# Who waits for the scatter of a mixture-of-experts stage: SyncE on one semaphore, or GpSimd on four

## The chip, the cores and the metric

One NeuronCore of a Trainium2 chip runs the whole program. The metric is the device time of one execution in microseconds. The kernel before takes 1391.34 us (median of 3 runs, 1389.32 to 1392.08).

## The reference, cut to what matters

Four layers run one after the other over 2048 tokens of width 256, each with layer norms and a residual around it: attention, a mixture of experts, a state-space layer, a feed-forward layer. The change is in the second one:

```
logits = flat @ router_w                       # 2048 x 64
_, topk_idx = top_k(logits + router_bias, 4)   # four experts per token
routed = sum over the 4 choices of share * expert(token)
shared = sum over s of (silu(flat @ swg[s]) * (flat @ swu[s])) @ swd[s]
out    = routed + shared
```

## The kernel before

`stage_moe` has two parts, `stage_route` and `stage_slots`, and each is one `nc.Block()`: five programs, one per engine, that run side by side and talk by semaphores. At the end of a block all engines meet: each drains and signals, GpSimd collects the signals of the other four after its own program has ended, and releases them. Line 782 is that of the route block, line 1169 that of the slots block.

In `stage_route` the 16 token tiles (`NT`) of 128 rows are normalised into `rows`, the router picks 4 experts (`TOPK`) per token, and VectorE works out in `find_slots` a row number for each of the 2048 x 4 choices, in four groups of tiles; each group raises `slots_ready`. GpSimd then copies the rows into the DRAM tensor `slots_in` (`xs` in the code), which SyncE had filled with zeros: 64 indirect DMAs (line 826), one per tile and choice, each of 128 rows of 1 KB. Each adds 16 to the semaphore `scattered`. These DMAs are the last work of GpSimd's program in this block. SyncE's program issues the constants' loads and nine blocks of zeros, and then waits until `scattered` is 1024 (line 790).

TensorE, ScalarE and VectorE meanwhile compute the shared experts: 16 steps of `hidden` (lines 897) into `pg` and `pu`, gate (line 967), product (line 1081), split (lines 971, 1085) and `down` (line 907) into `acc`. TensorE runs the first four steps as straight code and the other twelve as a loop of three passes (`repeat`); the other two engines have straight code throughout. Beside steps 3 to 6 VectorE also works out the shares (lines 1132 to 1135). ScalarE's copy of `acc` (line 960) ends the block.

In `stage_slots` SyncE first issues, with no wait of its own, three loads of `slots_in` (line 1185) and three of the experts' weights (line 1188). That they see the scattered rows rests on the block's end alone. GpSimd's first work there is a copy of weights (line 1179), after it has waited for the loads of all experts. Later, in `stage_mid`, GpSimd fetches the results by 64 indirect DMAs (line 1433), where every four that belong to one tile raise one semaphore of eight.

`chip.kept_sem` hands out the next number of a range of 40 semaphores that stay in use over the stages.

Of the kernel before, what the change touches and what calls it, by code (L numbers as in the profile page):

```python
# [17 lines left out]
NT = B * S // P  # L18
# [5 lines left out]
NE, FE, TOPK = 64, 64, 4  # L24
# [62 lines left out]
def linker(eng, sem):  # L87

    n = [0]

    def link(ins):
        n[0] += 1
        ins.then_inc(sem, 1)
        eng.wait_ge(sem, n[0])

    return link
# [593 lines left out]
def stage_moe(chip, x, y, ident, xs, xs_clear, fill, ys, t, ins):  # L690
    with ExitStack() as room:
        sb, _ = chip.memory(room)
        xh, xl = (sb(name, [P, KD, TOK], F32R) for name in ("xh", "xl"))
        rows = sb("rows", [P, NT, D])
        stage_route(chip, x, rows, xh, xl, y, ident, xs, xs_clear, fill, t, ins)
    with ExitStack() as room:
        sb, _ = chip.memory(room)
        weights = sb("weights", [P, NE, WEXP])
        stage_slots(chip, ident, xs, ys, weights, t, ins)


def stage_route(chip, x, rows, xh, xl, y, ident, xs, xs_clear, fill, t, ins):
# [10 lines left out]
    with ExitStack() as ctx:  # L713
# [55 lines left out]
        shifted, exp_done = chip.sem("shifted"), chip.sem("exp_done")  # L769
        chosen_done, ranks_done = chip.sem("chosen_done"), chip.sem("ranks_done")  # L770
        owner_found, owner_turned, owner_out = (chip.sem(n) for n in ("owner_found", "owner_turned", "owner_out"))
        slots_ready, scattered = chip.sem("slots_ready"), chip.kept_sem("scattered")
        s_loaded, none_set = chip.sem("s_loaded"), chip.sem("none_set")
        s_half, s_split = chip.sem("s_half"), chip.sem("s_split")
        gate_done, up_done, silu_done = chip.sem("gate_done"), chip.sem("up_done"), chip.sem("silu_done")
# [3 lines left out]
        def tiles(g):  # L779
            return slice(g * TPC, (g + 1) * TPC)  # L780

        with nc.Block() as block:
            @block.sync
            def _(sp):
                for dst, src in ((wraw, "router_w"), (bias, "router_b"), (sums, "sums"), (places, "places")):
                    sp.dma_start(dst[:], ins[src]).then_inc(loaded, 16)
                sp.dma_start(sraw[:], ins["shared_w"]).then_inc(s_loaded, 16)
                for part in fill[0]:
                    fill[1](sp, part)
                sp.wait_ge(scattered, NT * TOPK * 16)  # L790

            @block.gpsimd
            def _(pool):
                chip.clear_old()
                link = linker(pool, pool_link)
                nc.gpsimd.memset(none[:], 0.0).then_inc(none_set, 1)
                link(nc.gpsimd.memset(power[:], -0.5))
                pool.wait_ge(none_set, 1)

                def deviations(kind, g):  # L800
                    pool.wait_ge(var_ready, kind * NCH + g + 1)
                    link(nc.gpsimd.tensor_tensor(rstd[:, kind, tiles(g)], var[:, kind, tiles(g)], power[:], ALU.pow))
                    nc.gpsimd.tensor_tensor(shift[:, kind, tiles(g)], negmean[:, kind, tiles(g)],
                                            rstd[:, kind, tiles(g)], ALU.mult).then_inc(rstd_ready, 1)

                def split(s):
                    pool.wait_ge(s_loaded, 16)
                    nc.gpsimd.tensor_tensor(sh[:, s, :], sraw[:, s, :], none[:].broadcast_to([P, WBLK]),
                                            ALU.add).then_inc(s_half, 1)
                    pool.wait_ge(s_half, s + 1)  # L810
                    nc.gpsimd.tensor_tensor(sl[:, s, :], sraw[:, s, :], sh[:, s, :].bitcast(F32),
                                            ALU.subtract).then_inc(s_split, 1)

                for g in range(NCH):
                    deviations(OF_Y, g)
                for g in range(NCH):
                    deviations(OF_X, g)
                    if g >= 1:
                        split(g - 1)
                split(SHARED - 1)  # L820
                pool.wait_ge(xs_clear, BLANKS * 16)
                for g in range(NCH):
                    pool.wait_ge(slots_ready, g + 1)
                    for i in range(g * TPC, (g + 1) * TPC):
                        for k in range(TOPK):
                            nc.gpsimd.indirect_dma_start(  # L826
                                out=xs[:, :], out_offset=bass.IndirectOffsetOnAxis(slots[:, i, k:k + 1], 0),
                                in_=rows[:, i, :], in_offset=None).then_inc(scattered, 16)

            @block.tensor  # L830
            def _(pe):
# [1737 lines left out]
```

## Time and profile before

| what | value |
|---|---|
| median of 3 runs | 1391.34 us |
| lowest, highest | 1389.32, 1392.08 us |
| span of the profiled execution | 1441.3 us |
| TensorE busy in it | 1177.3 us, 82% |
| GpSimd busy in it | 369.6 us, 26% |
| mean granted clock of TensorE | 0.899 of full speed |

The page has no time of the profiled execution beside its span. The span is 50.0 us longer than the median of the runs, so a duration taken from the profile may be longer than in a timed run. In the rows below a time of the form "306.80 1.44" is a start and a duration in us, and the brackets behind a row give how long the engine was idle before it and what ended that.

### The profile page before, as it was taken

What the parts mean: (1) busy time and instruction counts of PE and PEld (TensorE: products, weight loads), DVE (VectorE), ACT (ScalarE), POOL (GpSimd) and SP (SyncE); (2) the same over time, 40 slices, a digit from 0 to 9 for tenths busy, and PEclk for the clock granted to TensorE, in tenths of its full rate; (3) what the DMA queues carried; (4) which work ended last, traced back from release to release, by engine and by line L of the source; (5) the groups of instructions that cost most, each with busy time, mean ns of one, the idle gap of its engine ahead of it and who ended that gap; (6) DMA issues with size and microseconds to landing.
All of it is one profiled execution on the core that took longest, in us unless ns stands there. A gap on an engine that the chain in (4) does not pass through costs nothing. (4 is left out here: it accounts for less than half of the span.)

```text
span 1441.3 us, 25339 instructions
## 1 busy us (share of the span) xinstructions
PE 1177.3 (82%) x9352; PEld 987.1 (68%) x9352; DVE 846.4 (59%) x1764; ACT 618.7 (43%) x1411; POOL 369.6 (26%) x467
## 2 busy tenths in 40 slices
PE   6579996672288999336779999999999999998896
PEld 5557774651177889324555888888888888886775
DVE  6456675871163566447836666656666665664364
ACT  5324443510033344125764554455455545553464
POOL 4321111637500025577304202300410050000111
PEclk9879999575589999758789999999999999999998
DMA  7934641612204997435324223332442232222001
GB/s 218 271 92 108 207 127 46 268 44 106 84 0 172 411 353 273 155 106 160 131 96 120 95 81 111 103 95 75 125 146 81 95 119 80 75 74 78 1 15 44
DMA packets 97540, 181.78 MB, mean 126 GB/s; under 512 B 11590, under 2 KB 49734, under 8 KB 94726
## 3 DMA queue, kind: packets, MB, share of 16 engines
q1 hardware_dynamic: 91148, 163.15, 33.8%
q0 software_dynamic: 6272, 17.05, 3.8%
q8 instruction: 73, 1.20, 0.3%
q14 instruction: 47, 0.39, 0.1%
HBM read 112.59 MB, written 67.37 MB: 125 GB/s over the span
## 5 line engine op out<-in xcount | busy, mean ns | idle before, releaser
L2020 ACT ACTIVATE decay<-masked,negcum 128x128 f32<-128x128 f32 x512 | 164.0, 391 | 241.0 <-issue 156.4
L2125 DVE COPY cT<-pcT 128x512 f32<-128x512 f32 x128 | 88.4, 690 | 174.4 <-PE pcT L1944 174.4
L1955 PEld LDWEIGHTS pcb<-cT,bT 128*128 128x128 f32 x1024 | 134.4, 191 | 10.6
L1955 PE MATMUL pcb<-cT,bT 128*128 128x128 f32 x1024 | 135.3, 275 | 0.0
L1882 POOL TENSOR_TENSOR wh<-wraw,none 128x512 fp32r<-128x512 f32 x32 | 35.1, 1096 | 318.2 <-DMA wraw<-in_w_bc 221.5
L1944 PE MATMUL pbT<-xh,wh 128*128 128x512 f32 x256 | 111.9, 437 | 1.1 <-POOL wl L1885 1.1
L2084 DVE TENSOR_TENSOR mixT<-pcb,decay 128x512 f32<-128x512 f32 x128 | 88.5, 691 | 23.0 <-PE pcb L1955 22.6
L1944 PE MATMUL pcT<-xh,wl 128*128 128x512 f32 x256 | 100.6, 393 | 0.0
L1944 PE MATMUL pbT<-xl,wh 128*128 128x512 f32 x256 | 100.1, 391 | 0.0
L1944 PE MATMUL pbT<-xh,wl 128*128 128x512 f32 x256 | 100.0, 390 | 0.0
L1944 PE MATMUL pcT<-xh,wh 128*128 128x512 f32 x256 | 99.7, 390 | 0.0
L1944 PE MATMUL pcT<-xl,wh 128*128 128x512 f32 x256 | 99.6, 389 | 0.0
L611 ACT ACTIVATE probT<-pst 128x384 f32<-128x384 f32 x128 | 61.7, 492 | 83.5 <-PE pst L545 78.3
L629 DVE TENSOR_REDUCE third<-ps 128x3 f32<-128x384 f32 x128 | 69.3, 548 | 47.3 <-PE ps L529 46.2
L2074 DVE TENSOR_TENSOR masked<-cumrow,mask 128x512 f32<-128x512 f32 x128 | 94.9, 742 | 0.0
L2039 ACT ACTIVATE bT<-pbT 128x512 f32<-128x512 f32 x128 | 74.5, 582 | 25.7 <-PE pbT L1944 25.6
L1433 POOL DMA_INDIRECT back<-slots_out,slots x64 | 67.7, 1058 | 29.0 <-issue 28.1
L1179 POOL COPY copies<-weights 128x384 f32 x64 | 32.5, 508 | 163.0 <-issue 142.1
L826 POOL DMA_INDIRECT slots_in<-rows,slots x64 | 62.6, 978 | 43.3 <-DVE slots L1067 24.1
L1308 DVE TENSOR_TENSOR hT<-gate,pgu 64x512 f32<-64x512 f32 x64 | 44.2, 691 | 29.4 <-ACT gate L1283 29.0
L1081 DVE TENSOR_TENSOR prod<-gate,pu 128x512 f32<-128x512 f32 x16 | 11.0, 686 | 78.5 <-remote 37.2
L2093 DVE TENSOR_TENSOR cS<-cT,grown 128x256 f32<-128x256 f32 x128 | 56.9, 444 | 0.1
(351 smaller groups left out, 3050.8 us busy)
## 6 DMA issues: line engine op xcount, KB each, us to landing
cumrow<-ssm_cum SPq DMA_DIRECT2D x128, 256.0 KB, 3.3
slots_in<-blank SPq DMA_DIRECT2D x16, 1024.0 KB, 10.8
xg<-slots_in SPq DMA_DIRECT2D x32, 512.0 KB, 6.3
slots_out<-yg SPq DMA_DIRECT2D x32, 512.0 KB, 3.4
stack<-qk_parts SPq DMA_DIRECT2D x32, 384.0 KB, 4.7
weights<-in_expert_quads SPq DMA_DIRECT2D x16, 768.0 KB, 10.1
wraw<-in_w_bc SPq DMA_DIRECT2D x32, 256.0 KB, 3.6
qk_parts<-parts SPq DMA_DIRECT2D x16, 384.0 KB, 2.6
```

The source lines that it names most:

```text
L611: nc.scalar.activation(probT[:, n % HELD, :], pst[n % T_BANKS][:, 0:3 * P], ACT.Exp).then_inc(exped, 1)
L629: nc.vector.tensor_reduce(third[:, u % 2, j, :], src, AX.X, ALU.max, negate=True).then_inc(maxed, 1)
L826: nc.gpsimd.indirect_dma_start(out=xs[:, :], out_offset=bass.IndirectOffsetOnAxis(slots[:, i, k:k + 1], 0), in_=rows[:, i, :], in_offset=N ...
L1433: nc.gpsimd.indirect_dma_start(out=back[:, i % BACK, k, :], out_offset=None, in_=ys[:, :], in_offset=bass.IndirectOffsetOnAxis(slots[:, i, ...
L1944: last = nc.tensor.matmul(bank[:], w[:, j, col:col + P], a[:, k, c * CHUNK:(c + 1) * CHUNK], start=(m == 0), stop=(m == len(parts) - 1))
L1955: last = nc.tensor.matmul(pcb[n % 2][:, o], bT[:, n % 2, o], cT[:, n % 2, o], start=True, stop=True)
L2020: last = nc.scalar.activation(decay[:, n % 2, o], masked[:, n % 2, o], ACT.Exp, bias=negcum[:, c * TPC + i, head:head + 1])
L2039: nc.scalar.activation(bT[:, n % 2, :], pbT[:], ACT.Copy).then_inc(b_out, 1)
L2074: nc.vector.tensor_tensor(masked[:, n % 2, :].rearrange("p (i l) -> p i l", l=P), cumrow[:, n % CUMS, :].rearrange("p (i l) -> p i l", l=P ...
L2084: nc.vector.tensor_tensor(mixT[:, n % KEEP, :], pcb[n % 2][:], decay[:, n % 2, :], ALU.mult).then_inc(mix_out, 1)
L2093: nc.vector.tensor_tensor(cS[:, n % KEEP, :, :], second, grown[:, n % 2, :, :], ALU.mult).then_inc(c_scaled, 1)
L2125: nc.vector.tensor_copy(cT[:, n % 2, :], pcT[:]).then_inc(c_out, 1)
```

## The change

The semaphore `scattered` becomes a list of four, one for each of a token's choices, and the DMA of choice `k` raises the `k`-th. Each of the four ends at 256 in place of one at 1024. SyncE's wait goes. GpSimd waits for all four at the end of its own program of this block.

```diff
-        slots_ready, scattered = chip.sem("slots_ready"), chip.kept_sem("scattered")
+        slots_ready = chip.sem("slots_ready")
+        scattered = [chip.kept_sem("scattered") for _ in range(TOPK)]
@@ sync
                 for part in fill[0]:
                     fill[1](sp, part)
-                sp.wait_ge(scattered, NT * TOPK * 16)
-
@@ gpsimd
                         for k in range(TOPK):
                             nc.gpsimd.indirect_dma_start(
                                 out=xs[:, :], out_offset=bass.IndirectOffsetOnAxis(slots[:, i, k:k + 1], 0),
-                                in_=rows[:, i, :], in_offset=None).then_inc(scattered, 16)
+                                in_=rows[:, i, :], in_offset=None).then_inc(scattered[k], 16)
+                for k in range(TOPK):
+                    pool.wait_ge(scattered[k], NT * 16)
```

## Rows read from the trace of the kernel before

**Rows 1.** The waits of SyncE's DMA queue: total us, times, longest.
```profile
SPq L782 <- DMA slots_in<-rows,slots: 137.6, 1, 137.6
SPq L782 <- PEq L782: 61.9, 1, 61.9
```
**Rows 2.** The timeline of SyncE's queue, 240 to 462 us: start, us, work.
```profile
246.78 5.63 SPq L2442 DMA_DIRECT2D slots_in<-blank  x9
452.23 0.32 SPq L1185 DMA_DIRECT2D xg<-slots_in  x1
```
**Rows 3.** The timeline of GpSimd, 250 to 462 us: its last work in this block.
```profile
306.80 1.44 POOL L826 DMA_INDIRECT slots_in<-rows,slots  x1 [24.14 <-DVE slots L1067]
...
309.83 0.96 POOL L826 DMA_INDIRECT slots_in<-rows,slots  x1 [0.30 <-issue]
311.09 0.96 POOL L826 DMA_INDIRECT slots_in<-rows,slots  x1 [0.30 <-issue]
...
387.64 0.96 POOL L826 DMA_INDIRECT slots_in<-rows,slots  x1 [0.30 <-issue]
```
**Rows 4.** The timeline of all engines, 384 to 462 us: VectorE's products, ScalarE's last copy.
```profile
397.82 0.69 DVE L1081 TENSOR_TENSOR prod<-gate,pu 128x512 f32<-128x512 f32 x1 [22.86 <-ACT gate L967]
...
403.58 0.69 DVE L1081 TENSOR_TENSOR prod<-gate,pu 128x512 f32<-128x512 f32 x1
...
409.34 0.69 DVE L1081 TENSOR_TENSOR prod<-gate,pu 128x512 f32<-128x512 f32 x1
...
450.88 1.08 ACT L960 ACTIVATE y<-acc 128x512 f32<-128x512 f32 x2 [2.50 <-PE acc L907]
```
**Rows 5.** The timeline of GpSimd in the stage before: one wait between two operations.
```profile
249.34 1.01 POOL L802 TENSOR_TENSOR rstd<-var,power 128x4 f32<-128x4 f32 x1 [0.93 <-DVE var L996]
250.43 0.20 POOL L803 TENSOR_TENSOR shift<-negmean,rstd 128x4 f32<-128x4 f32 x1
```
**Rows 6.** The timeline of GpSimd, 452 to 625 us: next block, then the gather.
```profile
520.72 0.51 POOL L1179 COPY copies<-weights 128x384 f32 x1 [132.12 <-issue]
...
594.91 1.01 POOL L1433 DMA_INDIRECT back<-slots_out,slots  x1 [10.81 <-issue]
...
600.00 1.69 POOL L1433 DMA_INDIRECT back<-slots_out,slots  x1 [0.30 <-issue]
...
606.55 0.95 POOL L1433 DMA_INDIRECT back<-slots_out,slots  x1 [0.30 <-issue]
607.80 0.95 POOL L1433 DMA_INDIRECT back<-slots_out,slots  x1 [0.30 <-issue]
...
613.07 0.95 POOL L1433 DMA_INDIRECT back<-slots_out,slots  x1 [0.30 <-issue]
```
**Rows 7.** Busy us of each engine (instructions) before, in and after the stretch from 331.8.
```profile
306.80:331.80 25.00, 15.97 (x65) 13.66 (x66) 18.91 (x55) 6.60 (x8) 19.21 (x20) 0.73 0.27 95
331.80:397.80 66.00, 11.79 (x33) 7.07 (x31) 5.19 (x6) 1.82 (x3) 43.39 (x45) 0.55 0.26 92
397.80:452.00 54.20, 49.91 (x272) 42.58 (x272) 27.49 (x34) 18.05 (x31) 0.00 (x0) 0.95 0.00 0
```
**Rows 8.** Who waited for whom, 331 to 398 us.
```profile
DVE prod L1081 <- remote: 37.2, 1, 37.2
...
PE pu L897 <- issue: 31.8, 1, 31.8
...
ACT gate L967 <- remote: 24.9, 1, 24.9
```
**Rows 9.** The indirect DMAs of the gather: duration ns min/median/max, first and last start.
```profile
L1433 POOL DMA_INDIRECT back<-slots_out,slots x64: 942/950/2989, 594.9 to 697.5; - x64
```
**Rows 10.** The page's DMA queues: packets, MB, share of 16 engines.
```profile
q8 instruction: 73, 1.20, 0.3%
```

## The prediction, made before the changed kernel had run

> **What bounds the kernel now.** I read the waits of SyncE's own queue first, because the change takes one of them away. SyncE waited 137.6 us for the scatter and then 61.9 us more for the end of the block, whose last signal came from TensorE's side [rows 1]. Its last DMA before these waits ended at 246.78 + 5.63 = 252.41 [rows 2]. So the scatter was complete at 252.41 + 137.6 = 390.0, and the block ended at 390.0 + 61.9 = 451.9. The timeline agrees: ScalarE's last copy ends at 450.88 + 1.08 = 451.96 [rows 4], and SyncE issues the next block's first load at 452.23 [rows 2]. GpSimd's timeline has its last indirect DMA at 387.64 for 0.96 us, ending at 388.6 [rows 3]; what it issued had landed 1.4 us later. What bounds this block is therefore the chain of shared-expert steps on TensorE, ScalarE and VectorE, with 61.9 us between the scatter's landing and the end of the block. I call these 61.9 us the cover.
>
> **The part that decides how much cover there is.** From 331.8 to 397.8 us the three computing engines do almost nothing: 11.79, 5.19 and 1.82 us of work on TensorE, VectorE and ScalarE in 66.0 us [rows 7]. The waits there have no engine as releaser: VectorE stood 37.2 us, TensorE 31.8 and ScalarE 24.9 [rows 8]. This stall lies wholly beside the scatter and ends shortly after it; the 25 us before have a scatter at the same DMA share (0.27 against 0.26) and no such stall [rows 7]. The work in that stretch is one step from product to product, which takes 409.34 - 403.58 = 5.8 us afterwards [rows 4]. So the stall is worth 66.0 - 5.8 = 60.2 us in the profiled execution. Its span is 1441.3 us and the median of the runs 1391.3, 50.0 us less; the page doesn't say where these 50 us are. If they are all in this stall, a timed run has a cover of 61.9 - 50.0 = 11.9 us. Had it no stall at all, the block would end at 451.9 - 60.2 = 391.7, and the cover would be 391.7 - 390.0 = 1.7 us. I keep all three: 61.9, 11.9 and 1.7.
>
> **SyncE's wait goes.** Nothing stands behind it in SyncE's program but the meeting at the block's end, and the next loads come after that meeting. Before, SyncE reached the meeting at 390.0; now it does so at 252.4. It then waits there for the others, until the same 451.9. Gain: 0, hidden by the shared experts. If the cover were gone, the gain would be the hop from SyncE to GpSimd, for which I take the same price as for a passed wait, below.
>
> **GpSimd waits four times.** Behind these waits on GpSimd are only its drain and its part of the meeting. The waits start at 388.6 and the last one is through when the last DMA has landed, at 390.0, as before; the first three are for DMAs issued up to 3 x 1.26 us earlier (the distance from 309.83 to 311.09 [rows 3]) and have passed by then or within the same microsecond. The trace has no row for a wait that passes at once. The nearest one is GpSimd's pair of operations with one such wait between them: 249.34 + 1.01 = 250.35 to 250.43, so 0.08 us [rows 5]. The other end is 0.30 us, the pause between two indirect DMAs, which has no wait in it [rows 3]; below, nothing. I take 0.08, since a wait is in that gap: 4 x 0.08 = 0.3 us, at most 1.2. GpSimd then stands ready at 390.3 (391.2 at most) for a meeting at 451.9. Cost: 0, and hidden even by the smallest cover of 1.7 us. GpSimd's next work after the meeting is at 520.72 [rows 6], so that its program is four instructions longer is hidden there too. Nobody waits for it in between: the meeting's release comes with TensorE's, VectorE's and ScalarE's arrival.
>
> **Four semaphores in place of one.** The 64 DMAs are the same, in the same order, with the same 1024 counts in sum. What may differ is the cost of naming another semaphore than the DMA before. The scatter of before always names the same one, so I take the gather, where every fourth indirect DMA changes it. Its first 16 start at 594.91; the changes fall on the 5th, 9th and 13th: 600.00 took 1.69 us, 607.80 took 0.95 and 613.07 took 0.95, with 0.95 at 606.55, where nothing changes [rows 6]. The gather's median is 950 ns [rows 9], the scatter's plain rows 0.96 [rows 3]. The upper bound is 1.69 - 0.95 = 0.74 us on each of 63 changes, 46.6 us; the lower one is the gather's minimum against the scatter's row, 64 x (0.942 - 0.96) = -1.2 us. Two of three changes cost nothing, so I take 0. Even the upper bound would be hidden by the cover of 61.9 us, but not by that of 11.9: 46.6 - 11.9 = 34.7 us.
>
> **The sum.** 0 (SyncE) + 0 (GpSimd's waits) + 0 (four semaphores) = 0. Against the profiled execution that is a span of 1441.3 us; carried to the median of the runs, 1391.3 us. A difference of under 0.2% (2.8 us) can't be told from none here, and the three runs of before differ by that much themselves.
>
> **A rule on the program's code.** Instructions reach the core as data too: 73 packets with 1.20 MB, 16.4 KB each [rows 10], and GpSimd's program is longer by four waits, SyncE's shorter by one, so the places where a new piece is needed move by that much on these two engines and not on the other three. The longest idle time of GpSimd outside the scatter that neither an engine nor a DMA ended, with work of its own next, is 10.81 us ahead of the gather [rows 6]. It holds the change of block too, so it is an upper bound for such a load. Taken once, in full, and on the path, it is worth 10.8 us in either direction.
> The Trainium skill, page "Runtime: NRT & Kernel Launch", section "Instruction fetch mechanics", says that code is streamed in blocks of 16 KiB, 256 instructions, and that crossing into the next one is mostly hidden. By it this edit costs 0. The trace agrees on the size (16.4 KB a packet) and leaves the "mostly" open, because TensorE, VectorE and ScalarE stood for 24.9 to 37.2 us with no engine to wait for [rows 8].
>
> **The rivals.**
> - *The stall gets shorter (faster).* If what holds the three engines from 331.8 on were the counts arriving at one semaphore on which SyncE is parked, four semaphores with nobody parked on them would free them. For it: the stall lies beside the scatter, and no engine releases it [rows 7, 8]. Against it: the 25 us before have the same scatter, the same parked SyncE and 15.97 us of TensorE's work [rows 7]. Its worth is at most 60.2 us, to 1331 us; if the 50.0 us of the profiled span are in it already, 10.2 us remain: 1381 us.
> - *Naming another semaphore costs (slower).* Each indirect DMA takes up to 0.74 us more, the scatter lands up to 46.6 us later, and GpSimd's last wait becomes what ends the block. It decides only from the point where the scatter grows by more than the cover. With 11.9 us of cover the time is 1391.3 + 34.7 = 1426 us; at 0.2 us a DMA it is 12.6 - 11.9, nothing. For it: one change at 1.69 us; against it: the two at 0.95 [rows 6].
> - *A piece of code comes at another moment.* GpSimd or SyncE, a few instructions off, runs out of code at a place where others wait for it, or no longer does. 1391.3 + 10.8 = 1402 us, or 1391.3 - 10.8 = 1380.5 us.
> - *The change isn't what it seems.* If SyncE kept its wait, the result would be 0 as well.
>
> **How the numbers follow.** No change by over 0.2%: 0.72, at 1391.3 us, with 1388.5 to 1394.1 as its own range. A shorter stall: 0.07. Costly semaphores: 0.05. Code at another moment: 0.16, half in each direction. Faster is 0.07 + 0.08 = 0.15, the same 0.72, slower 0.05 + 0.08 = 0.13. The range takes in most of the moved code's case, which is rarely worth its full 10.8 us, and leaves the stall and the costly semaphores outside: 1383 to 1399 us.
>
> **What would show each step.** SyncE's queue should have no wait for the scatter, and one of about 199.5 us (137.6 + 61.9) for the block's end. GpSimd's indirect DMAs should keep 0.96 us and 0.30 us of pause, the last starting near 387.6. ScalarE's copy should still end the block, near 452. VectorE's wait of about 37 us should be there again. The prediction is wrong if the product that comes at 397.82 is more than 3 us earlier or later counted from the scatter's first DMA, if the pause or length of the indirect DMAs grows, or if a stage after 452 us changes its length.

## The result, and the profile after

Over 17 runs each the changed kernel takes 1394.97 us (1391.75 to 1397.59) and the kernel before 1391.84 us (1387.59 to 1396.27), a ratio of 1.002 with a 95% interval of 1.0011 to 1.003: slower by 1.5 to 4.2 us. The forecast was no change. The measured time lies inside the range of 1383 to 1399 us, but the change is clear of its noise and was given a chance of 13%.

The first line of the changed kernel's page, and its row for the scatter (busy us, mean ns of one, idle us before):

```profile
span 1391.4 us, 25341 instructions
...
L825 POOL DMA_INDIRECT slots_in<-rows,slots x64 | 67.8, 1059 | 43.4 <-DVE slots L1068 24.2
```

The span is 49.9 us shorter than that of the profile of before. This isn't the change's doing: the kernel before takes 1391.84 us in this comparison too. The largest wait from 300 to 452 us of the changed kernel:

```profile
ACT hh L972 <- DVE prod L1082: 47.6, 16, 8.0
```

It is made of 16 short waits with VectorE as releaser. Nowhere in the list does VectorE, TensorE or ScalarE stand for 25 to 37 us with no engine as releaser, as in [rows 8]. The stall on which the largest cover of the forecast rested is missing in this execution. The end of the block, in the timeline of all engines (start, us, work), to be held against [rows 2 to 4]:

```profile
394.30 1.09 ACT L961 ACTIVATE y<-acc 128x512 f32<-128x512 f32 x2 [2.50 <-PE acc L908]
...
396.19 0.96 POOL L825 DMA_INDIRECT slots_in<-rows,slots  x1 [0.30 <-issue]
...
404.39 0.32 SPq L1186 DMA_DIRECT2D xg<-slots_in  x1
```

ScalarE's last copy ends at 395.39, GpSimd's last indirect DMA at 397.15, and SyncE's first load of the next block comes at 404.39. So 7.24 us pass after the last indirect DMA although TensorE, VectorE and ScalarE are done. SyncE's queue has one wait where it had two [rows 1], as the change says:

```profile
SPq L783 <- PEq L783: 148.0, 1, 148.0
```

The view names TensorE's queue (PEq) as releaser of the meeting here as in [rows 1]. That name can't be relied on: in this execution GpSimd was the last to arrive, as the records below show.

### The profile page after: what moved, and what is told of

The parts are those of the page before. It is cut to its first block and busy times, and to the rows that moved or that the text cites. A ratio compares the mean times of both kernels' runs of the same rounds, so it can differ in the third digit from the quotient of the medians.

```text
span 1391.4 us, 25341 instructions
## 1 busy us (share of the span) xinstructions
PE 1164.5 (84%) x9352; PEld 980.0 (70%) x9352; DVE 845.4 (61%) x1764; ACT 618.2 (44%) x1411; POOL 375.1 (27%) x467
## 5 line engine op out<-in xcount | busy, mean ns | idle before, releaser
L2021 ACT ACTIVATE decay<-masked,negcum 128x128 f32<-128x128 f32 x512 | 164.0, 391 | 240.9 <-issue 156.3
L2085 DVE TENSOR_TENSOR mixT<-pcb,decay 128x512 f32<-128x512 f32 x128 | 88.5, 692 | 22.9 <-PE pcb L1956 22.6
L825 POOL DMA_INDIRECT slots_in<-rows,slots x64 | 67.8, 1059 | 43.4 <-DVE slots L1068 24.2
L1945 PEld LDWEIGHTS pbT<-xh,wh 128*128 128x128 f32 x256 | 48.4, 189 | 11.7 <-issue 4.8
```

What stands on the lines that cost most here:

```text
L825: nc.gpsimd.indirect_dma_start(out=xs[:, :], out_offset=bass.IndirectOffsetOnAxis(slots[:, i, k:k + 1], 0), in_=rows[:, i, :], in_offset=N ...
L1945: last = nc.tensor.matmul(bank[:], w[:, j, col:col + P], a[:, k, c * CHUNK:(c + 1) * CHUNK], start=(m == 0), stop=(m == len(parts) - 1))
L2021: last = nc.scalar.activation(decay[:, n % 2, o], masked[:, n % 2, o], ACT.Exp, bias=negcum[:, c * TPC + i, head:head + 1])
L2085: nc.vector.tensor_tensor(mixT[:, n % KEEP, :], pcb[n % 2][:], decay[:, n % 2, :], ALU.mult).then_inc(mix_out, 1)
```

## The experiments

The two theories. **E**: what counts is who waits. GpSimd has work of its own at the block's end, its drain (the instruction at the end of its program; in every block of these traces it ends after GpSimd's last operation); with the wait on SyncE this runs beside the landing of the rows, with the wait on GpSimd it runs behind it. **F**: what counts is the four semaphores.

**e1 to e4: the change taken apart.** e1 is the kernel before, e4 the changed kernel. e2:

```diff
-                sp.wait_ge(scattered, NT * TOPK * 16)      # sync
+                pool.wait_ge(scattered, NT * TOPK * 16)    # gpsimd, behind the scatter
```

e3 (the DMA of choice `k` raises `scattered[k]`, as in the changed kernel; that line is left out here):

```diff
+        scattered = [chip.kept_sem("scattered") for _ in range(TOPK)]
-                sp.wait_ge(scattered, NT * TOPK * 16)
+                for k in range(TOPK):
+                    sp.wait_ge(scattered[k], NT * 16)
```

Expected of e1: 

> The kernel before, unchanged, for a second profile of it. The profile of the changed kernel shows no stall of the three computing engines beside the scatter, and its span (1391.4 us) is that of its timed runs, so theory H (the stall belongs to some executions, not to either kernel's code) expects either outcome here; if the stall is missing, the span is 1385 to 1395 us, the shared experts end about 144 us after SyncE's first load of the block (as in the changed kernel, 395.4 - 247.8 = 147.6, or a little less), and the distance from the end of GpSimd's last indirect DMA to the next block's first load is visible for the first time. Theory E (that distance is 7.2 us in the changed kernel, 397.15 to 404.39, because GpSimd itself is the one that waits, so that what it does at the block's end comes after the landing and not beside it) expects 3 to 5 us here. Theory F (four semaphores make the scatter longer or its landing later) expects about 7 us minus nothing for the waits but a last indirect DMA that ends earlier. Time: ratio 1.000.

Expected of e2: 

> Half of the change: one semaphore as before, but GpSimd waits for it at the end of its program, and SyncE doesn't. Theory E (who waits matters): slower than before by about 0.2%, 3 us, like the changed kernel, with 6 to 7 us from the last indirect DMA to the next block's first load. Theory F (the four semaphores matter): the same as before, ratio 1.000.

Expected of e3: 

> The other half: four semaphores, one per choice, but SyncE waits for all four, and GpSimd for none. Theory E: the same as before, ratio 1.000, 3 to 5 us from the last indirect DMA to the next block's first load. Theory F: slower by about 0.2%, 3 us.

Expected of e4: 

> The changed kernel again, beside the two halves on the same chip. Both theories: 1.002 of before, 3 us. If its profile has the stall this time, the stall belongs to the execution and not to the change; if it has none, the end of the block shows the distance of 7.2 us again.

Measured: 1445.16, 1445.82, 1446.14 and 1444.07 us, ratios of 1.0006, 1.0005, 1.0008 and 1.0001 to the kernel before (1444.86 us there), each interval within 0.9991 to 1.002. On this chip every kernel, the one before included, takes some 53 us more than in the first comparison, and the stall is in all four profiles. The expectation of 1.002 for e4 and, by either theory, for one of e2 and e3 was missed. Of e1, 331 to 398 us:

```profile
DVE prod L1081 <- remote: 35.7, 1, 35.7
```

With the stall the next block begins 62 to 64 us after the scatter, and neither half of the change shows in the time. The intervals alone don't exclude 1.65 us (they reach up to 1.002, which is 2.9 us); the traces do, since GpSimd is done at least 55.9 us before ScalarE. That is what the prediction's cover of 61.9 us says.

The views leave drains and semaphore instructions out, but the trace has records of them. From these, for every kernel of which a profile was taken, in us counted from the end of the last indirect DMA of the scatter:

```
kernel                      drain of GpSimd  it     it ends  ScalarE's   next block's
                            starts           takes           copy ends   first load
before (stall)              -15.16           20.45   5.29     63.36       63.63
e1  before (stall)          -15.15           20.45   5.30     62.40       62.67
e2  one sem., GpSimd waits    1.64            5.28   6.92     62.80       63.06
e3  four, SyncE waits       -15.15           20.45   5.30     63.20       63.46
e4  changed (stall)           1.72            5.29   7.01     62.92       63.18
changed (no stall)            1.71            5.29   7.00     -1.77        7.24
e5  cut, before             -15.15           20.45   5.30      9.63        9.90
e6  cut, one, GpSimd          1.64            5.28   6.92      9.15        9.41
e7  cut, four, SyncE        -15.19           20.49   5.30      8.66        8.92
e8  cut, changed              1.72            5.29   7.01      9.70        9.96
e9  late, before            -15.15           20.45   5.30    -41.06        5.54
e10 late, one, GpSimd         1.66            5.28   6.94    -42.14        7.18
e11 late, four, SyncE       -15.12           20.42   5.30    -40.46        5.54
e12 late, changed             1.71            5.29   7.00    -41.63        7.23
e13 late, then 16 copies      9.24            5.28  14.52    -39.92       14.77
e14 late, then a memset     -13.89           19.30   5.41    -40.49        5.65
e15 before (stall)          -15.18           20.48   5.30     62.47       62.73
e16 changed (stall)           1.72            5.29   7.00     62.90       63.16
e17 pause, before           -15.10           20.40   5.30    -24.46        5.54
e18 before (no stall)       -16.40           21.69   5.29     -1.76        5.54
```

The columns on the drain are the finding. Where SyncE waits and nothing stands behind the DMAs, GpSimd's sequencer (the part that reads its instructions) enters the drain 15 to 16 us before the last indirect DMA has run, and the drain ends 5.3 us after that DMA. Where GpSimd waits, the drain starts only after the rows have landed. The last count of the last DMA arrives 1.45 us after its end (e10, e18 and the changed kernel); the drain starts at 1.64 to 1.72, once the waits are passed, and takes 5.28 us from there. The wait puts the landing and the drain one after the other.

**e5 to e8: the cover taken away by cutting work.** Twelve of the 16 shared-expert steps are left out of each of the four:

```diff
-    STEPS = SHARED * NCH
+    STEPS = SHARED
-                repeat(pe, NCH, body)
+                body(0)
```

Expected of e5: 

> The kernel before with 12 of the 16 shared-expert steps left out (12 of 16 tiles' shared part isn't added), so that the scatter ends the block whether or not the three computing engines stall beside it. On the chip of e1 to e4 the stall was there in all four kernels and gave a cover of 61 us, and all four were the same (ratios 1.0001 to 1.0008), while on the chip of the first comparison the changed kernel's profile had no stall and 3 us more. So the price should show where the cover is taken away. All theories: about 1445 - 58 = 1387 us where the stall is, about 1385 where it isn't. The distance from the end of GpSimd's last indirect DMA to the next block's first load: theory E (GpSimd's end of program runs beside the landing when SyncE waits, and behind it when GpSimd waits) 3 to 5 us; theory F (four semaphores) 7 us here as well, the scatter itself being shorter than in the changed kernel.

Expected of e6: 

> The same cut, with one semaphore on which GpSimd waits. Theory E: 2 to 4 us more than e5, all of it between the last indirect DMA's end and the next block's first load (7.2 us). Theory F: as e5 within 0.5 us in that distance.

Expected of e7: 

> The same cut, with four semaphores on which SyncE waits. Theory E: as e5 within 0.5 us. Theory F: 2 to 4 us more than e5, in the scatter (64 indirect DMAs) or after it.

Expected of e8: 

> The same cut of the changed kernel. Theory E: as e6, plus three more passed waits (0.1 to 0.3 us). Theory F: as e7. Neither: as e5, and the 3 us of the first comparison come from somewhere else.

Measured: 1393.04, 1393.41, 1393.64 and 1392.78 us, no difference between the four (the kernel before took 1447.55 us there, and 1387 were expected of e5). The cut didn't do what I wanted: ScalarE, which had one copy left to do, came out of the stall only after the scatter. Of e5:

```profile
399.83 1.08 ACT L960 ACTIVATE y<-acc 128x512 f32<-128x512 f32 x2 [25.29 <-remote]
```

Its end at 400.91, not GpSimd, let the block end. Counted from the last indirect DMA it varied by 1 us between the four. As a test of time these runs are inconclusive; the drains in the table repeat those of e1 to e4.

**e9 to e12: the scatter made late.** GpSimd makes 128 copies into a spare tile ahead of the last 16 indirect DMAs. The output is unchanged, and the scatter now ends behind the shared experts, stall or not:

```diff
+                    if g == NCH - 1:
+                        for _ in range(128):
+                            link(nc.gpsimd.tensor_copy(filler[:], flat(rows[:, 0:2, :])[:, 0:384]))
```

Expected of e9: 

> The kernel before, with 128 copies on GpSimd (128x384, 0.6 us each with their link, about 75 us) put ahead of the last 16 of the 64 indirect DMAs, so that the scatter ends near 465 us, behind the shared experts on any chip, with or without the stall. Nothing of the output changes. In e1 to e8 GpSimd's drain at the block's end shows in the trace: where SyncE waits it begins while the DMAs are still being issued and ends 5.29 us after the last one, where GpSimd waits it begins when the rows have landed, 1.6 to 1.7 us after the last one, and takes 5.28 us more. Theory E: from the end of the last indirect DMA to the next block's first load 5.3 + 0.3 = 5.6 us here. Theory F: 7.2 us here as well, or a longer scatter in e11.

Expected of e10: 

> The same delay, with one semaphore on which GpSimd waits. Theory E: 7.2 us from the last indirect DMA to the next block's first load, 1.6 us more than e9, and the time 1.6 us above e9's. Theory F: as e9.

Expected of e11: 

> The same delay, with four semaphores on which SyncE waits. Theory E: 5.6 us and the time of e9. Theory F: 1.6 us or more above e9.

Expected of e12: 

> The same delay in the changed kernel. Theory E: 7.2 us, as e10, with at most 0.3 us for the other three waits. Theory F: as e11. If e10 and e12 are above e9 by 1.6 us and not by 3, the rest of the first comparison's 3 us isn't in the block's end.

The last indirect DMA and the next block's first load, in the timelines of GpSimd and SyncE; first e9, where SyncE waits:

```profile
471.90 0.96 POOL L830 DMA_INDIRECT slots_in<-rows,slots  x1 [0.30 <-issue]
...
478.40 0.32 SPq L1189 DMA_DIRECT2D xg<-slots_in  x1
```

e10, one semaphore and GpSimd waits:

```profile
472.82 0.96 POOL L829 DMA_INDIRECT slots_in<-rows,slots  x1 [0.30 <-issue]
...
480.95 0.32 SPq L1189 DMA_DIRECT2D xg<-slots_in  x1
```

e11, four semaphores and SyncE waits:

```profile
471.07 0.96 POOL L832 DMA_INDIRECT slots_in<-rows,slots  x1 [0.30 <-issue]
...
477.57 0.33 SPq L1191 DMA_DIRECT2D xg<-slots_in  x1
```

In e12, the changed kernel, they come at 471.41 and 479.61. The distances from the DMA's end to the load are 5.54, 7.18, 5.54 and 7.23 us: 1.64 us for the wait's place and 0.05 us for three more waits, as theory E said to 0.1 us, and nothing for the four semaphores where SyncE waits. Theory F, which wanted the price in e11 and none in e10, falls. The times are 1469.42, 1471.14, 1472.28 and 1472.57 us (5 runs each; ratios to before 1.0163, 1.0175, 1.0182 and 1.0191, intervals of 0.0018 to 0.0025 to either side, which overlap). e10 is 1.72 us over e9, near the expected 1.6, e12 3.15 and e11 2.86. e11's difference has no counterpart in this block: from its first to the end of its last indirect DMA e11 took 164.75 us and e9 167.03. I don't read it as a price of the four semaphores, and can't exclude one of 2 us outside this block by these times alone. These medians of five runs are too rough for a price of 1.65 us; the distances in the traces carry it.

**e13 and e14: what the drain's 5.28 us belong to.** e9 with 16 copies, and e9 with one small memset, between the last indirect DMA and the end of GpSimd's program:

```diff
+                for _ in range(16):                                          # e13
+                    link(nc.gpsimd.tensor_copy(filler[:], flat(rows[:, 0:2, :])[:, 0:384]))
+                nc.gpsimd.memset(filler[:, 0:1], 0.0)                        # e14
```

Expected of e13: 

> e9 (late scatter, one semaphore, SyncE waits) with 16 copies on GpSimd behind the last indirect DMA, about 10 us. If the drain's price is fixed (theory D1), it ends 5.3 us after the last copy and the next block's first load comes 5.5 us after it, so 15 us after the last indirect DMA. If the 5.28 us belong to DMAs just ahead of the drain (theory D2), the drain ends with or shortly after the last copy, and the load comes within 1 us of it.

Expected of e14: 

> e9 with one memset of 128 elements on GpSimd behind the last indirect DMA. D1: the next block's first load 5.54 us after the last DMA as in e9, or 0.1 to 0.2 us later. D2: 2 to 3 us after it, since then only the landing (1.64 us) counts.

Of each of the two there is one run, the profiled one; their times are not used.

GpSimd and SyncE in e13:

```profile
476.15 9.05 POOL L834 COPY filler<-rows 128x384 f32<-128x384 f32 x16
...
490.92 0.32 SPq L1191 DMA_DIRECT2D xg<-slots_in  x1
```

In e14:

```profile
471.45 0.12 POOL L833 MEMSET filler<- 128x1 f32 x1
...
477.10 0.32 SPq L1190 DMA_DIRECT2D xg<-slots_in  x1
```

The load comes 490.92 - 485.20 = 5.72 us after the last copy and 477.10 - 471.57 = 5.53 us after the memset. So the drain ends 5.3 to 5.5 us after GpSimd's last operation, with either of these between it and the DMAs, and 9 us of distance from them don't shorten it: theory D1 holds, D2 falls, and no better kernel comes of a small operation there. One thing more from the trace's records of the changed kernel, of all its blocks. In the five others in which GpSimd issued no DMA its drains took 0.30 to 2.98 us, and each of them ended 0.05 to 0.07 us after GpSimd's last operation: the longer ones began while GpSimd still had operations to run. In the block of the gather, where GpSimd issued 64 indirect DMAs and then four plain ones, the drain took 6.14 us and ended 5.62 us after the last of these. So the price goes with blocks in which GpSimd issued DMAs. Whether with their number, or with indirect ones alone, wasn't tried.

**e15 and e16: the pair again.** Expected of e15: 

> The kernel before again, for its profile on a chip without the stall, if this is one. Then the last indirect DMA should end at or after the shared experts (as in the changed kernel, 397.15 against 395.4), and the next block's first load should come 5.54 us after it. With the stall: 62 to 64 us after it, the time at 1445 us.

Expected of e16: 

> The changed kernel beside it. Without the stall: the first load 7.24 us after the last indirect DMA and 1.7 us over e15 by the block's end; if the time is 3 us over, the other half comes from elsewhere, and the two profiles will show from which stage. With the stall: the same as before, 1.000.

Measured: 1443.63 and 1444.39 us, ratios of 0.999 (0.9974 to 1.0006) and 0.9992 (0.9978 to 1.0007). With the stall again, and the same again; the next load came 62.73 and 63.16 us after the last indirect DMA.

**e17: a pause in the scatter.** The kernel before with 32 copies ahead of the 25th indirect DMA:

```diff
+                        if i == 6:
+                            for _ in range(32):
+                                link(nc.gpsimd.tensor_copy(filler[:], flat(rows[:, 0:2, :])[:, 0:384]))
```

Expected: 

> The kernel before with a pause of 32 copies on GpSimd (128x384, about 18 us) ahead of the 25th indirect DMA, about 337 to 355 us, shortly after the stall's start at 332. Theory S1 (the stall of TensorE, VectorE and ScalarE is held up by the indirect DMAs being issued): the three go on within a few us of the pause's start, the stall shrinks from 60 us to under 25, the shared experts end near 415 and the scatter, 18 us late, near 408; on a chip with the stall the time falls by 30 to 40 us, to 1405 to 1415 (ratio 0.975). Theory S2 (the stall has another cause, such as the age of what the engines wait for): no change in the waits of 37, 32 and 25 us, and a ratio of 1.000, since the scatter has a cover of 61 us. Without the stall on this chip: about 18 us slower than before.

This chip had no stall: the kernel before took 1392.62 us, so the run can't decide between S1 and S2. (The traces of e9 to e14 can, see "What stays open".) But it settles another thing. The pause came out at 25.9 us where 18 were expected, and the kernel took 1414.97 us, ratio 1.0162 (1.0141 to 1.0183): 22.4 us more. The chain in its timelines, from the pause through ScalarE's last copy to the next block:

```profile
339.55 25.87 POOL L828 COPY filler<-rows 128x384 f32<-128x384 f32 x32
...
393.27 1.08 ACT L964 ACTIVATE y<-acc 128x512 f32<-128x512 f32 x2 [2.50 <-PE acc L911]
...
417.86 0.96 POOL L830 DMA_INDIRECT slots_in<-rows,slots  x1 [0.30 <-issue]
...
424.36 0.33 SPq L1189 DMA_DIRECT2D xg<-slots_in  x1
```

From the scatter's first DMA the shared experts end after 86.7 us, against 85.3 in e18, and the scatter after 111.2 against 87.0. This delay of 24.2 us appears in the time as 22.4 (19.6 to 25.5), in full within the interval: without the stall the scatter is what bounds this block, and the cover is none.

**e18: the kernel before without the stall.** Expected: 

> The kernel before, once more, for a profile without the stall. e17's chip had none (before at 1392.6 us), SyncE's wait there ended and the next load came 5.54 us after the last indirect DMA, and a scatter held up by 22 us made the program 22 us longer. If this chip is like it: span near 1390 us, first load 5.54 us after the last indirect DMA, and from the first indirect DMA to that load about 92.5 us, 1.7 us under the changed kernel's 94.2 (310.19 to 404.39). If the scatter itself has another length than the changed kernel's 86.96 us (310.19 to 397.15), that is where the rest of the 3 us is. With the stall: 1445 us and 62 to 64 us, as in e1 and e15.

It took 1393.01 us beside 1392.33 for the same kernel. Its timelines:

```profile
309.85 1.44 POOL L826 DMA_INDIRECT slots_in<-rows,slots  x1 [24.12 <-DVE slots L1067]
...
395.90 0.96 POOL L826 DMA_INDIRECT slots_in<-rows,slots  x1 [0.30 <-issue]
...
394.01 1.09 ACT L960 ACTIVATE y<-acc 128x512 f32<-128x512 f32 x2 [2.50 <-PE acc L907]
...
402.40 0.33 SPq L1185 DMA_DIRECT2D xg<-slots_in  x1
```

And the two waits of SyncE's queue, which answer to [rows 1]:

```profile
SPq L782 <- DMA slots_in<-rows,slots: 142.8, 1, 142.8
...
SPq L782 <- PEq L782: 3.8, 1, 3.8
```

Held against the changed kernel's profile, which is of another chip: from the first indirect DMA's start to the last one's 395.90 - 309.85 = 86.05 us against 396.19 - 310.19 = 86.00; from the last one's start to the next load 6.50 against 8.20; in sum 92.55 against 94.20. So 1.65 us are lost in sum, after the last indirect DMA and not in the scatter.

## Why the prediction was wrong, point by point

**SyncE's wait goes: right.** It ended nothing. In e18, SyncE still waits 3.8 us after the rows have landed: for GpSimd's drain. The prediction read the last signal of before as TensorE's from the name in [rows 1]; the records have TensorE's drain end at 450.9 and ScalarE's at 452.0, so ScalarE was the last. Nothing in the sum hangs on this.

**Four semaphores: right.** The indirect DMAs keep 0.96 us and 0.30 us of pause in both kernels, and 86.0 us from the first to the last (e18 and the changed kernel). The rival "naming another semaphore costs" falls (e3, e11).

**GpSimd waits four times: the step that failed.** The prediction said that behind these waits stand "only its drain and its part of the meeting", priced the passed waits at 0.3 us and had GpSimd ready at 390.3. The passed waits were small, as forecast (0.05 us for three more of them, e10 against e12). The drain was given nothing. It takes 5.28 us, and in the kernel before it had begun 15 us early, so that GpSimd was ready 5.3 us after the last indirect DMA; with the wait ahead of it, 7.0 us after. The term is 1.65 to 1.7 us in place of 0, where it isn't covered. The views of before couldn't show the drain, because SyncE's 61.9 us for the meeting hid it completely; I took what was hidden for free.

**The cover: wrong where it mattered.** The prediction held GpSimd's cost hidden even by its smallest cover. Of its three covers (61.9, 11.9, 1.7 us) the runs of the first comparison had none: in the changed kernel ScalarE ends 1.77 us before the last indirect DMA, and e18 has 1.76 us for the kernel before. The reconstruction without the stall put the shared experts' end at 391.7 and the landing at 390.0, 1.7 us apart. In e18 ScalarE ends at 395.10, the last indirect DMA ends at 396.86, and GpSimd's drain 5.29 us later: GpSimd is 7.1 us the later one. Of these 8.8 us, 3.9 are the drain, which ends 5.3 us beyond the last DMA where I had 1.4 for the landing. Most of the rest is the scatter itself, which I had taken from the profile with the stall: 67.8 us busy against 62.6, since without the stall ten indirect DMAs take 1.36 to 1.68 us. The stall's worth was right: counted from the scatter's first DMA ScalarE ends after 145.2 us in the first profile and after 85.3 in e18, 59.9 us apart, forecast 60.2. The cover of 11.9 us assumed that 50.0 of these were gone and 10.2 left. All of them were gone, and the block became only 52.9 us shorter, because GpSimd took over its end.

**The signs that the prediction named.** Most of them failed in the changed kernel's profile. SyncE has one wait, but of 148.0 us and not 199.5; the last indirect DMA starts at 396.19 and not near 387.6; ScalarE's copy doesn't end the block; and VectorE's wait of 37 us isn't there. The missing stall explains these, and e18 shows the same without the change. None of the signs looks at GpSimd's drain.

**The stall rival, with its 60 us: not the change's.** The stall is in the kernel before and in the changed one alike (e1 to e4, e15, e16; the variants e5 to e14 have it too) and, by times and profiles, in neither on the chips of e17, of e18 and of the first comparison. It went with the chip or the session, 1444 to 1448 us against 1392 for the same kernel, and decided the result: with it the ratio was 1.0001 and 0.9992 for the changed kernel, without it 1.002.

**A piece of code at another moment: nothing of it seen.** From the next block's first load to the gather's first DMA 142.21 us in e18 and 142.58 in the changed kernel. The blocks further on are up to 2.5 us shorter in the changed kernel's profile; two profiles of the kernel before differ as much (161.7 us in e1 and 164.0 in e18 for the gather's block).

**What stays open.** The block's end explains 1.65 us of the measured 3.1; the interval, 1.5 to 4.2, holds it. No stage shows the rest: stages that the change doesn't touch differ by more from one execution to the next (SyncE's first load of this block comes at 247.5 in e18, at 247.8 in the changed kernel and at 244.5 in the first profile).

What ends the stall can be read from runs made for another purpose. In e9 to e14 the scatter pauses after its 48th indirect DMA. In the seven profiles with the stall and an unbroken scatter (the first one, e1 to e4, e15, e16) VectorE's fifth product starts 8.3 to 9.2 us after the end of the last indirect DMA, at 397.82 in [rows 4], behind a second wait of 22.9 us. In e9, whose pause starts at 367.27:

```profile
367.27 85.36 POOL L827 COPY filler<-rows 128x384 f32<-128x384 f32 x128
...
375.92 0.69 DVE L1085 TENSOR_TENSOR prod<-gate,pu 128x512 f32<-128x512 f32 x1
...
430.71 1.08 ACT L964 ACTIVATE y<-acc 128x512 f32<-128x512 f32 x2 [2.74 <-PE acc L911]
```

The second wait is gone. In e9 to e14 that product starts 6.7 to 9.9 us after the end of the 48th indirect DMA, and from the scatter's first DMA the shared experts take 124.3 to 127.3 us against 144.9 to 145.2 in those seven. That is 18 to 21 us less, for 16 indirect DMAs at a distance of 1.26 us that came later. So the second part of the stall goes on while indirect DMAs run and ends some 7 to 10 us after them, as theory S1 has it and S2 doesn't; GpSimd's copies don't keep it up. Of the first part, the wait of 30 to 40 us, these runs say nothing: it ends at 361 to 374 us in both groups. It suggests that the 61.9 us weren't a cover that a longer scatter could use up, since the stall would grow with it; no run lengthened the scatter on such a chip. How the stall begins, and why on some chips only, stays open. In the first profile a semaphore wait of VectorE stood for 38.3 us, to 369.1, although the matmuls of TensorE for which it waited are recorded as over at 329.7.

## What to carry to other kernels

A wait is cheap, but not where an engine would otherwise have gone on to something of its own: put a wait for DMAs on an engine with nothing to finish, not ahead of the drain of the engine that issued them. Here that is worth 1.65 us of 1392. A cover that comes from a stall isn't a cover: ask what ends last when the stall is gone, and count every engine's own end, drain included. And when a profile's span is 50 us from the median of the runs, it is the profile of another execution than the ones that are compared.

## What the runs showed of the hardware

- GpSimd's drain takes 5.28 us at the end of a block in which it issued 64 indirect DMAs, when it starts 1.7 us (e2, e10) or 9.2 us (e13) behind them; entered earlier, it ends 5.3 us after the last one (e9, e18). In the gather's block it ended 5.62 us after GpSimd's last DMA, and in the five other blocks, without DMAs of GpSimd, 0.05 to 0.07 us after its last operation.
- GpSimd's sequencer enters that drain some 15 us before the last indirect DMA has run, with twelve of them still to start. A wait in between takes this lead away.
- The last count of the last indirect DMA arrives 1.45 us after the instruction's end; a drain behind the wait for it starts at 1.64 us with one semaphore and at 1.72 with four.
- Without the stall, beside the shared experts, ten of the 64 indirect DMAs take 1.36 to 1.68 us in place of 0.96, 5.2 us over the 64 (e18 and the changed kernel against the first profile).
- The same program takes 1392 us on some chips and 1445 on others, from one stall of three engines beside the scatter, whose second part ends 7 to 10 us after an unbroken run of indirect DMAs does (e1 to e4, e9 to e16).
